# Five operand transposes of a round: from TensorE to SP's DMA queue, as 2-byte transposes of float16 halves

## The reference, cut to what matters

```python
nx = _ln(x, ln1_g, ln1_b)
q, k, v = nx @ wq + bq, nx @ wk + bk, nx @ wv + bv            # 8 heads of 32
attn = softmax(q k^T / sqrt(32) + where(adj > 0, 0.1*adj*adj, -inf))
x1 = x + ((attn @ v) @ wo + bo)
x = x1 + gelu(_ln(x1, ln2_g, ln2_b) @ w1 + b1) @ w2 + b2
for k in range(2):                                            # the two small layers
    q, kk = x @ Wq[k].T + bq[k], x @ Wk[k].T + bk[k]          # 128 columns
    attn = masked_softmax(q kk^T / sqrt(128))
    x = layer_norm(x + (attn @ x) @ Wc[k].T, ln_g[k], ln_b[k])
```

## Time and profile before

| | |
|---|---|
| median of 3 runs | 2197.3 us (2193.87 to 2198.27) |
| the profiled execution's own time | 2195.11 us |
| its span, first to last instruction | 2193.1 us |
| TensorE busy | 2016.2 us (92% of the span) |
| VectorE busy | 1721.4 us (78%) |
| ScalarE busy | 1558.7 us (71%) |
| GpSimd busy | 961.0 us (44%) |
| mean granted TensorE clock | 0.971 of full speed |

### The profile page before, as it was taken

How to read it: one execution, slowest core, us unless ns; L and a number is a source line. 1 busy time by engine, 2 the same in 40 slices (tenths; PEclk the granted TensorE clock), 3 DMA queues, 4 the chain that set the end, 5 groups by cost and what they waited for, 6 DMA issues and landing times.

```text
span 2193.1 us, 45905 instructions
## 1 busy us (share of the span) xinstructions
PE 2016.2 (92%) x16984; PEld 1499.2 (68%) x16984; DVE 1721.4 (78%) x3397; ACT 1558.7 (71%) x2994; POOL 961.0 (44%) x1304
## 2 busy tenths in 40 slices
PE   5589899999999999999999999999999999999853
PEld 4356677777777777777777777777777777777531
DVE  4566788888888888888888888888888888887422
ACT  2367777777788777777787777777877777777521
POOL 2022344445454454444554544445545444544434
PEclk8799999999999999999999999999999999999976
DMA  3211012222211122222111222222111222210000
GB/s 106 73 49 42 28 45 58 59 59 56 58 49 42 33 59 59 59 59 54 49 42 35 57 58 59 59 54 57 43 39 44 59 59 59 54 50 16 15 10 19
DMA packets 103675, 108.62 MB, mean 50 GB/s; under 512 B 9824, under 2 KB 78432, under 8 KB 103456
## 3 DMA queue, kind: packets, MB, share of 16 engines
q1 hardware_dynamic: 102912, 104.90, 17.9%
q0 software_dynamic: 544, 0.80, 0.2%
HBM read 38.55 MB, written 16.78 MB: 25 GB/s over the span
## 4 chain that ended last, share of the span: by engine, by line
PE 72%; ACT 13%; DVE 6%; POOL 4%; issue 3%; DMA 2%; SPq 1%; DVEq 0%; POOLq 0%; ACTq 0%
PE ps L243 18%; PE ps L245 17%; PE ps L244 17%; PE ps L812 5%; PE ps L972 5%; PE ps L1046 5%; ACT area L483 4%; PE ps L1026 3%; POOL x L403 3%; ACT cs L525 2%; DMA out<-x 2%; ACT area L533 2%; ACT L525 2%; PE ps L965 1%; ACT cq L518 1%
## 5 line engine op out<-in xcount | busy, mean ns | idle before, releaser
L483 ACT ACTIVATE area<-area,nmax 128x128 f32<-128x128 f32 x1024 | 312.5, 390 | 0.8
L243 PE MATMUL ps<-w_h,hid_h 128*128 128x256 f16 x1024 | 279.1, 273 | 6.0 <-POOL hid_l L250 5.1
L245 PE MATMUL ps<-w_h,hid_l 128*128 128x256 f16 x1024 | 279.0, 272 | 0.0
L244 PE MATMUL ps<-w_l,hid_h 128*128 128x256 f16 x1024 | 279.0, 272 | 0.0
L396 POOL TENSOR_TENSOR ve<-mv,eps_cols 128x4 f32<-128x4 f32 x128 | 25.7, 201 | 572.0 <-DVE mv L572 572.0
L250 POOL TENSOR_TENSOR hid_l<-area,hid_h 128x512 f16<-128x512 f32 x128 | 151.8, 1186 | 251.9 <-ACT hid_h L506 251.9
L503 ACT ACTIVATE area<-ps,b_col 128x512 f32<-128x512 f32 x256 | 176.3, 689 | 77.9 <-PE ps L245 76.8
L403 POOL TENSOR_TENSOR x<-xh,cg_row 128x256 f32<-128x256 f32 x128 | 89.0, 728 | 295.7 <-DMA out<-x 272.6
L243 PE MATMUL ps<-rot_h,w_h 128*128 128x512 f16 x512 | 194.4, 380 | 6.2 <-ACT area L503 2.9
L245 PE MATMUL ps<-rot_h,w_l 128*128 128x512 f16 x512 | 194.0, 379 | 0.0
L244 PE MATMUL ps<-rot_l,w_h 128*128 128x512 f16 x512 | 193.9, 379 | 0.0
(11 more groups left out here) (178 smaller groups left out, 6214.0 us busy)
## 6 DMA issues: line engine op xcount, KB each, us to landing
qkS<-qk SPq DMA_DIRECT2D x384, 128.0 KB, 2.4
xin<-in_x SPq DMA_DIRECT2D x32, 512.0 KB, 3.8
adj_in<-in_adj SPq DMA_DIRECT2D x64, 256.0 KB, 2.9
out<-x SPq DMA_DIRECT2D x32, 512.0 KB, 3.9
area<-in_L_gnn_w SPq DMA_DIRECT2D x2, 1024.0 KB, 11.3
area<-in_L_gnn_Wc SPq DMA_DIRECT2D x2, 256.0 KB, 11.3
area<-in_L_gnn_wq SPq DMA_DIRECT2D x1, 256.0 KB, 3.7
area<-in_L_gnn_wk SPq DMA_DIRECT2D x1, 256.0 KB, 4.0
```

What stands on the lines that cost most here:

```text
L243: pe.matmul(dst, lh, rh, start=start, stop=False, **kw)
L244: pe.matmul(dst, lh, rl, start=False, stop=False, **kw)
L245: return pe.matmul(dst, ll, rh, start=False, stop=stop, **kw)
L483: last = act.activation(sc[:, b % 2, h], sc[:, b % 2, h], ACT.Exp, bias=nmax[:, b, h:h + 1])
```

## The change

The eight transposes on TensorE are gone from all five places. ScalarE now copies the float32 rows in SBUF to a float16 tile with the nodes still on the partitions (`sN_h`, `sA_h`, `sC_h`), VectorE makes the low half from the same rows (`sN_l`, `sA_l`, `sC_l`), and SP turns each half with one DMA transpose of 128x1024 float16 elements (256 KB). TensorE waits for the DMAs (`m_xT`, `m_oT`, `m_mT`, `m_cT`, 32 for the two halves). All five order lists are written anew; their lines are left out but for the new `SYNC`.

```diff
-SYNC = ["Q.stk-2", "N.ld-1", "Q.ldA-1", "M.ldC-3", "C1.sto-6"]
+SYNC = ["A.oT-1", "C1.xT-4", "Q.stk+0", "N.ld+1", "M.mT-1", "C0.xT-2", "N.xT+1", "M.ldC-2",
+        "Q.ldA+1", "C1.sto-4"]
...
+        sN_h, sN_l = sb("sN_h", [P, KC, B, P], F16), sb("sN_l", [P, KC, B, P], F16)
+        sA_h, sA_l = sb("sA_h", [P, KC, B, P], F16), sb("sA_l", [P, KC, B, P], F16)
+        sC_h, sC_l = sb("sC_h", [P, KC, B, P], F16), sb("sC_l", [P, KC, B, P], F16)
...
+        TURN = 2 * 16
+        def by_chunk(rows):
+            return rows.rearrange("p b (c d) -> p c b d", c=KC)
...
+            def turn(g, dst_h, dst_l, src_h, src_l, a_made, d_made, m_done):
+
+                need_apart(sp, a_made, g, 1, 1)
+                sp.dma_start_transpose(dst_h.rearrange("p c (b t) -> p (c b) t", t=P),
+                                       src_h.rearrange("p c b d -> p (c b d)")).then_inc(m_done, 16)
+                need_apart(sp, d_made, g, 1, 1)
+                sp.dma_start_transpose(dst_l.rearrange("p c (b t) -> p (c b) t", t=P),
+                                       src_l.rearrange("p c b d -> p (c b d)")).then_inc(m_done, 16)
...
+                    if what == "xT" and stage == "N":
+
+                        for used in (*t_qk, *t_v):
+                            need_apart(sp, used, g, 1, 0)
+                        turn(g, xT_h, xT_l, sN_h, sN_l, a_xT, d_xT, m_xT)
+                    elif what == "oT":
+
+                        need_apart(sp, t_up, g, FC, 0)
+                        turn(g, rot_h, rot_l, sA_h, sA_l, a_oT, d_oT, m_oT)
+                    elif what == "mT":
+
+                        need_apart(sp, t_wo, g, 1, 1)
+                        turn(g, rot_h, rot_l, sA_h, sA_l, a_mT, d_mT, m_mT)
...
                     elif what == "oT":
-                        need(act, t_oT, g, 1, 1)
-                        need(act, t_up, g, FC, 0)
-                        act.copy(rot_h[:, :, :], psA).then_inc(a_oT, 1)
+                        need(act, d_o, g, B, B)
+                        need(act, m_mT, g, TURN, 0)
+                        act.copy(sA_h[:, :, :, :], by_chunk(o_rows)).then_inc(a_oT, 1)
...
                     elif what == "oT":
                         need(dve, a_oT, g, 1, 1)
-                        dve.tensor_tensor(rot_l[:, :, :], psA, rot_h[:, :, :], ALU.subtract)\
+                        need(dve, m_mT, g, TURN, 0)
+                        dve.tensor_tensor(sA_l[:, :, :, :], by_chunk(o_rows), sA_h[:, :, :, :], ALU.subtract)\
                            .then_inc(d_oT, 1)
...
-            def transposes(dst, rows, signal):
-
-                for c in range(KC):
-                    for b in range(B):
-                        last = pe.transpose(dst[:, c, b * P:(b + 1) * P], rows[:, b, c * P:(c + 1) * P],
-                                            ident[:, :])
-                last.then_inc(signal, 1)
...
-                    elif what == "oT":
-                        need(pe, d_o, g, B, B)
-                        transposes(psA, o_rows, t_oT)
                     elif what == "wo":
-                        need(pe, d_oT, g, 1, 1)
+                        need(pe, m_oT, g, TURN, TURN)
                         for b in range(B):
                             last = to_rows(psA_rows[:, b], rot_h, rot_l, wo_h, wo_l, b)
```

More of the change, by code:

```diff
@@ L463, in iteration @@
                     if stage == "N":
[L464 to L467, removed]
+                        need(act, d_xh[0], g, 1, 1)
+                        need(act, m_xT, g, TURN, 0)
+                        act.copy(sN_h[:, :, :, :], by_chunk(xhatN)).then_inc(a_xT, 1)
                     elif what in QK:
@@ L509, in iteration @@
                         if what == "xT":
-                            need(act, t_cT[l], g, 1, 1)
-                            need(act, t_cW[1 - l], g, 1, -1 if l == 0 else 2)
-                            act.copy(cT_h[:, :, :], psC).then_inc(a_cT[l], 1)
+                            if l == 0:
+                                need(act, d_x2, g, 1, 1)
+                                need(act, m_cT[1], g, TURN, -TURN)
+                            else:
+                                need(act, d_xh[2], g, 1, 1)
+                                need(act, m_cT[0], g, TURN, 2 * TURN)
+                            act.copy(sC_h[:, :, :, :], by_chunk((x2, xh3[:, :, :])[l])).then_inc(a_cT[l], 1)
                         elif what in ("q", "k"):
@@ L875, in iteration @@
                         freed(g, (a_gelu, 2, 8, 7), (d_v[1], 1, 1, 1))
-                    elif step == "C0.S":
-                        freed(g, (a_cq[0], 0, 1, 1))
                     elif step == "A.AV0":
@@ L881, in iteration @@
                         freed(g, (d_S, 0, 4, 4))
+                    elif step == "A.AV1":
+                        freed(g, (d_o, 0, 4, 1))
+                    elif step == "Q.k1":
+                        freed(g, (d_qk[1], 0, 1, 1))
+                    elif step == "A.AV2":
+                        freed(g, (d_o, 0, 4, 2))
+                    elif step == "A.PT3":
+                        freed(g, (d_PT, 0, 4, 3))
                     elif step == "C0.xW":
@@ L911, in iteration @@
+                    elif step == "C0.PV":
+                        freed(g, (a_cPT[0], 0, 1, 1))
+                        freed(g, (a_cW[0], 0, 1, 1))
+                    elif step == "A.wo":
+                        freed(g, (d_PT, 0, 4, 4))
+                    elif step == "C1.q":
+                        freed(g, (d_cy[0], -1, 1, 1), (d_cy[1], 1, 1, 1))
+                    elif step == "Q.v1":
+                        freed(g, (a_gelu, 2, 8, 8), (d_qk[3], 0, 1, 1))
                     elif step == "C1.k":
-                        freed(g, (d_cy[0], -1, 1, 1), (d_cT[1], 0, 1, 1))
-                    elif step == "C1.q":
-                        freed(g, (d_cy[0], -1, 1, 1), (d_cT[1], 0, 1, 1))
+                        freed(g, (d_cy[0], -1, 1, 1), (d_cy[1], 1, 1, 1))
+                    elif step == "C1.S":
+                        freed(g, (a_cq[1], 0, 1, 1))
@@ L933, in iteration @@
                         freed(g, (d_v[1], -1, 1, 1), (a_gelu, 1, 8, 8))
-                    elif step == "A.PT0":
-                        freed(g, (d_S, 0, 4, 2))
+                    elif step == "A.S1":
+                        freed(g, (d_S, 0, 4, 1))
                     elif step == "C1.PV":
@@ L991, in iteration @@
                         last.then_inc(t_wo, 1)
-                    elif what == "mT":
-                        need(pe, d_xh[1], g, 1, 1)
-                        transposes(psM, xhat, t_mT)
                     elif what[:2] == "up":
-                        need(pe, d_mT, g, 1, 1)
+                        need(pe, m_mT, g, TURN, TURN)
                         to_columns(psUp, w1_h, w1_l, rot_h, rot_l, b * P).then_inc(t_up, 1)
@@ L1010, in iteration @@
                         l = int(stage[1])
-                        if what == "xT":
-                            if l == 0:
-                                need(pe, d_x2, g, 1, 1)
-                            else:
-                                need(pe, d_xh[2], g, 1, 1)
-                            transposes(psC, (x2, xh3)[l], t_cT[l])
-                        elif what in ("q", "k"):
+                        if what in ("q", "k"):
                             i = "qk".index(what)
-                            need(pe, d_cT[l], g, 1, 1)
+                            need(pe, m_cT[l], g, TURN, TURN)
                             to_columns(psC[:, i, :], cqk_h[:, l], cqk_l[:, l], cT_h, cT_l, i * P)\
```

135 lines of the change are left out of this document (59 added, 76 removed), and 30 rows, old and new, of tables (SCALAR, TENSOR, VECTOR).

## The result

The changed kernel takes 2179.2 us (median of 4 runs, 2176.41 to 2180.93), the kernel before 2195.7 beside it: a ratio of 0.992, 95% interval 0.991 to 0.993. It is 16.5 us faster; 61 were forecast.

A forecast was written before the change was run, and what follows sets the result against it. TensorE was taken to bound the kernel: 4.4 us of transposes less 1.2 for new waits and 1.3 for slip gives 1.9 us a round, 61 us over 32 rounds, so 2135 us from 2195; range 2085 to 2270 us.

The forecast's parts named there:

- TensorE is the bound: Even stretch: TensorE busy 61.2 of 62.4 us a round, so removing five transpose steps frees 4.4 us a round.
- what the new order gives back: TensorE's new waits around C1.S, C1.xW and C1.PT: 0.4, 0.5 and 0.3 us, together 1.2 us a round lost.
- h and L: One DMA transpose on SP: h, its hold of the queue, taken as 1.5 us; L, issue to landing, 4.0 us.
- block by block: Rival: a DMA transpose handled as eight separate blocks, h 5.3 and L 7.0 us; about 2800 us; 12% with all above 2270.
- x + 3h + 9.7: When Q.stk has landed for A.S0, after A.oT's low half is made; x is h - 1.3, or 0 if negative.
- `A.S0` late: A.S0 on TensorE, due at 12.6 us, gets Q.stk at 14.4: 1.8 us late, 1.3 taken as slip a round.
- The clock: TensorE's clock: read as fully granted in the profile before; no loss counted for the changed kernel.
- `C1.PV`: C1.PV on TensorE: counted as 1.73 us of products, with no wait of its own.
- Handing over at `C1.S`: C1.S right behind C1.k on TensorE waits 1.0 us for ScalarE's ck, 0.4 more than before.
- The turns with room: C0.xT and N.xT: over 10 us of TensorE's work between operand and reader, so no delay.
- nothing that counts: Work added on ScalarE and VectorE by reading SBUF: 0.03 to 0.04 us five times a round, 0.2 us on each engine.
- SP's queue is held longer: Rival: Q.stk comes too late for A.S0; gain gone at h = 2.0 us; 2200 to 2270 us, 15%.

The follow-up runs named there:

- e10: The kernel before, with two float16 products in place of the eight float32 transposes in each of five steps, no DMA added: 2188.5 us, 0.995.
- e5: The kernel before, with only N.xT turned through SP's queue and the rest in its old order: 2204.7 us, 1.004.
- e6: The changed kernel with Q.stk's twelve DMAs split, six ahead of the transposes, and Q.v0 moved ahead of C1.xW on TensorE: 2145.1 us, 0.977.
- e3: The changed kernel with nine filler products on TensorE right ahead of A.S0, their result overwritten: 2156.4 us, 0.981.
- e1: The changed kernel with six of Q.stk's twelve DMAs issued ahead of the transposes: 2150.6 us, 0.978.
- e12: e6 with plain DMAs of the same 256 KB instead of the DMA transposes, so operands are not turned: 2144.0 us, 0.977.
- e4: The changed kernel with one more DMA transpose, of a tile nobody reads, ahead of Q.stk in SP's queue: 2234.0 us, 1.016.
- e13: e6 with A.S1 moved ahead of C1.PT and M.up1 ahead of C1.PV on TensorE: 2183.6 us, 0.993.

## Why the prediction was wrong

The sign and the range held; 61 us were forecast and 16.5 came.

**The step that failed is the first: "TensorE is the bound ... what TensorE no longer does is gained until something else holds it up", and with it the term of 1.2 us for what the new order gives back.** e10 takes out half of the 4.4 us and gets 10 us of 70, none of them in the even stretch. e5 takes out a fifth and gets slower, in part by a late DMA. The kernel before had many short waits between in-order steps, of 0.2 to 0.4 us where they could be seen, and by the estimate above 2.5 us a round of lost time, where the prediction had 1.2 of idle time. That the transposes covered latencies is shown for the five together by e10; it was not tested one by one. In the prediction's sum this is the price of the new waits: 1.2 us forecast, 2.7 in e6, where neither SP's queue nor the clock adds to it.

**Part of the 16.5 us is luck.** The 1.9 us forecast were for a round, and a round got 0.2. Of the 14 us between the two profiled executions 10 lie in the drain, which the prediction counted as rounds.

**h and L: the main doubt, and both came out better.** h is 1.24 to 1.35 us (1.5 taken), L is 2.8 (4.0 taken). The rival "block by block" fell: eight times the 1309 ns that the Trainium skill, page "VectorE: DVE Perf Modes", section "The three transpose paths", gives for one block would be 10.5 us, and the trace has 2.8 for all eight. (The prediction took its own 7.0 and this 10.5 for one and the same.) The 261 GB/s for DMA transposes of the Trainium skill, page "DMA: Bandwidth & Descriptors", section "Latency and other measured facts", make 1.0 us of transfer, an estimate; a plain copy of the size landed in 2.3 us and the transpose in 2.8, which does not speak against it. With the measured h and L the prediction's own frame gives: `A.S0` at x + 3h + 9.7 = 13.8 against 12.6, a slip of 1.2 - 0.5 = 0.7, and 4.4 - 1.2 - 0.7 = 2.5 us a round. Measured was 0.2. The 2.3 us between, term by term (each is read by itself, so that they nearly add up is a check and no proof):

- **`A.S0` late: 1.2 worked out, 1.97 measured**, 0.8 more. In the order of time of the 18 rounds `Q.stk` starts 4.8 us behind the low half of `A.oT` on average, where 4.1 were worked out, since it starts 0.65 us behind the end of the last transpose. `A.S0` runs 10.1 us behind that start (9.7 worked out), and without the wait would have run at 12.9 (12.6). The burst of twelve itself is no longer than before.
- **The clock: put at nothing**, 1.1 (e3). "At the full granted clock" was read from before and carried over to a kernel with longer waits.
- **`C1.PV`: put at nothing**, 0.59. It was treated as having no operand that could be late.
- **Handing over at `C1.S`: right.** 1.0 us of wait and drain were forecast, 0.87 of wait measured. The wait of `C1.PT`, 0.3, did not come here; nor did that of `C1.xW`, 0.5, which the prediction had already set against the slip of `A.S0`. `A.S0` was late by more than both; they came in e1 and e6.

0.8 + 1.1 + 0.6 - 0.3 = 2.2 of the 2.3.

**Give-back.** The 1.2 us for new waits is too small also where nothing else is in the way. In e6, whose 1100 us from 540 to 1640 hold 18.1 rounds, the three waits are 66.3 us, 3.7 a round, against 1.0 of all waits before. Of the 4.4 us 1.7 stay, a round of 60.7 us; waits for a DMA are 0.3 us in all 18 rounds, and e12 shows that shorter holds and landings give nothing more.

**The turns with room** (`A.wo`, `C0.xT`, `N.xT`) had it, as worked out; `M.up0` waits in 2 of 18 rounds. **VectorE and ScalarE**: "nothing that counts" held for the engines' sum (54.0 and 48.4 us a round, 53.5 and 48.3 before), but not for one row:

```profile
L738 DVE TENSOR_TENSOR sA_l<-area,sA_h x19: 1224/1687/1825, 528.3 to 1647.6; 128x1024 f16<-128x1024 f32 x19
```

```profile
L755 DVE TENSOR_TENSOR sA_l<-area,sA_h x19: 1215/1216/1216, 545.0 to 1664.1; 128x1024 f16<-128x1024 f32 x19
```

The same operation on the same shapes takes 1687 ns (median) for `A.oT` and 1216 for `M.mT`. It delays the low half of `A.oT`, and with it all of SP's queue behind, by up to 0.6 us. What lies beside it is GpSimd. In all 19 rounds an addition of GpSimd (line 439) overlaps the subtraction for `A.oT`, and in none that for `M.mT`. Two of them, each with its neighbour:

```profile
842.30 0.73 POOL L439 TENSOR_TENSOR x<-x,cb_row 128x256 f32<-128x256 f32 x1
842.32 1.79 DVE L738 TENSOR_TENSOR sA_l<-area,sA_h 128x1024 f16<-128x1024 f32 x1 [1.11 <-ACT sA_h L528]
```

```profile
905.62 1.23 DVE L738 TENSOR_TENSOR sA_l<-area,sA_h 128x1024 f16<-128x1024 f32 x1 [1.11 <-ACT sA_h L528]
905.69 1.74 POOL L439 TENSOR_TENSOR x<-x,cb_row 128x256 f32<-128x256 f32 x1
```

Where the addition had begun first, the subtraction is the longer one and ends 1.08 us behind the addition's end; where an addition began behind the subtraction, as in the second pair, the subtraction keeps its 1.23 us and that addition takes 1.74 instead of 0.73. So these two hold each other up. (In one round the addition began 8 ns behind the subtraction and still went first.) No run moved one of them, so what it costs the round is not known.

**Rivals.** "SP's queue is held longer" was the right mechanism at a smaller h: the edge is steep (e4: 1.7 us for one more hold), and the change stands on it. **What stays open:** the one loop, if it is one, that gives the kernel before its 62.4 us. e10 shows that the sum of TensorE's work does not set it; the waits that grew there are for ScalarE, GpSimd and VectorE, but no run took one of these latencies away alone.

## What to carry to other kernels

Before counting work that leaves the busiest engine as gained, cut it down in place, with nothing added, and time that: one such run (e10) would have put the ceiling of this change in doubt at the start. In an in-order list a step is also cover for the latency of its neighbours; whoever takes it out has to put the order right again, and look for what shares a bank (e13) or a queue (e1, e4) with what moves up. When a DMA is put ahead of a long burst in the same queue, split the burst.

## What was not expected of the hardware

- A DMA transpose of 128x1024 2-byte elements between SBUF tiles holds SP's queue for 1.24 us and lands 2.8 us after its issue; a plain copy of the same 256 KB holds 0.47 and lands after 2.3.
- TensorE's clock fell to its lower level for some 3.4 us behind idle times of 0.87 and 2.37 us, both between 666.0 and 670.4, and in 14 of 18 rounds at this place. Nine filler products in the second of them kept it up, for 1.1 us a round; a useful step there kept it up in most rounds.
- Twelve plain DMAs held SP as long beside 94 GB/s of traffic in the DMA engines as beside 52: 8.0 and 8.4 us on average, 0.60 us for one in the median.
- A subtraction of VectorE (128x1024, both inputs in SBUF) and an addition of GpSimd (128x256) did not run side by side: with one exception in 19 rounds the one that began second took longer, 1.79 us instead of 1.22, or 1.74 instead of 0.73.
